# A graph network kernel: superblocks of destination nodes summed in pairs, and a fourteenth one by counted cells

## The reference, cut to what matters

```
msg = x[src] @ W_msg.T + b_msg + edge_embed[edge_type]
messages = segment_sum(msg, dst)             # (12500, 128)
x = layernorm(x + gru_cell(messages, x))     # W_ih, W_hh, b_ih, b_hh
h = x
for each of 3 layers:                        # with edge attributes, 16 wide
    agg = segment_sum(h[src] (+ or concat) (edge_attr @ enc_w + enc_b), dst)
    h = relu(bn(agg @ w1 + b1)) @ w2 + b2
out = layernorm(x + h)
```

## Time and profile before

| | |
|---|---|
| median of three runs | 7135.25 us |
| the profiled execution, and its span | 7139.24 us, 7137.2 us |
| share of the span busy | PE 82%, POOL 71%, DVE 46%, ACT 19% |
| busy tenths of PE in 40 slices | 2577777666677377767599999999999999999999 |
| busy tenths of the DMA engines in 40 slices | 6699999999999433333477778778878888778776 |

### The profile page before, as it was taken

The page is one execution under the profiler, slowest core; times in us unless marked ns, Lnnn a source line. Parts: engine busy times, 40 slices in busy tenths (PEclk is TensorE's granted clock), DMA queues, the critical chain, the costliest instruction groups (busy, mean ns, idle before and its releaser), DMA issues.

```text
span 7137.2 us, 82504 instructions
## 1 busy us (share of the span) xinstructions
PE 5870.9 (82%) x29016; PEld 2854.1 (40%) x29152; DVE 3267.2 (46%) x8030; ACT 1370.1 (19%) x2496; POOL 5097.1 (71%) x4958
## 2 busy tenths in 40 slices
PE   2577777666677377767599999999999999999999
PEld 1233333333333143333344444444455444445444
DVE  5666666655565486676544444432222222222222
ACT  1233333333334121121111111110000000000000
POOL 3766666666667477777577777777777777777775
PEclk9998898888989587777699999999999999999999
DMA  6699999999999433333477778778878888778776
GB/s 222 161 238 245 236 240 239 244 240 243 250 242 254 121 99 97 99 99 98 137 240 240 236 229 247 236 242 258 243 233 254 245 243 269 240 241 241 242 240 191
DMA packets 1463508, 1536.87 MB, mean 215 GB/s; under 512 B 820755, under 2 KB 1202772, under 8 KB 1463100
## 3 DMA queue, kind: packets, MB, share of 16 engines
q1 hardware_dynamic: 1250604, 1182.45, 58.4%
q0 software_dynamic: 212496, 349.08, 19.2%
HBM read 1082.27 MB, written 281.76 MB: 191 GB/s over the span
## 4 chain that ended last, share of the span: by engine, by line
PE 53%; POOL 5%; DVE 3%; DMA 2%; issue 2%; ACT 1%; SPq 0%; ACTq 0%; DVEq 0%
PE ps L2502 34%; PE ps L2473 6%; POOL BIG L2556 5%; PE ps L2447 2%; PE ps L2446 2%; PE ps L2359 1%; PE ps L2431 1%; PE ps L2360 1%; PE ps L2453 1%; DMA XT<-rec_q 1%; PE ps L2454 1%; PE ps L2398 1%; DVE BIG L1883 1%; PE ps L2361 1%; DMA RECL<-rec_q 1%
## 5 line engine op out<-in xcount | busy, mean ns | idle before, releaser
L2574 POOL DMA_INDIRECT GL<-h_gathered,IDXA x2646 | 2700.7, 1021 | 919.5 <-issue 770.4
L2502 PE MATMUL ps<-MS,HP 128*128 128x512 bf16 (+1 forms) x11700 | 2712.0, 376 | 27.8 <-DMA MS<-counts 16.1
L2541 POOL DMA_INDIRECT rec_q<-BIG x1563 | 1562.7, 1000 | 777.5 <-issue 470.2
L2502 PEld LDWEIGHTS ps<-MS,HP 128*128 128x128 bf16 x11700 | 1132.7, 98 | 1251.9 <-issue 117.1
L2300 PE MATMUL ps<-MT,XPS 128*128 128x512 bf16 x3763 | 1082.7, 397 | 490.8 <-ACT MT L2102 281.0
L2556 POOL DMA_INDIRECT BIG<-x_parts,SRCq x739 | 828.9, 1122 | 290.1 <-issue 222.8
L2102 ACT CAST MT<-ps 128x512 bf16<-128x512 f32 x1274 | 735.9, 586 | 971.3 <-PE ps L2286 823.9
L1960 DVE TENSOR_REDUCE ROW<-ps 128x128 f32<-128x384 f32 x294 | 163.0, 554 | 1517.6 <-PE ps L2473 1517.6
L2300 PEld LDWEIGHTS ps<-MT,XPS 128*128 128x128 bf16 x3822 | 373.7, 101 | 983.9 <-ACT MT L2102 433.5
L2473 PE MATMUL ps<-GL,SL 128*128 128x384 bf16 (+1 forms) x2646 | 593.9, 333 | 26.0 <-DVE SL L1926 26.0
L2286 PE MATMUL ps<-BIG 128*128 128x512 bf16 x1197 | 470.1, 393 | 44.6 <-DVE BIG L1748 30.1
(11 more groups left out here) (198 smaller groups left out, 4982.6 us busy)
## 6 DMA issues: line engine op xcount, KB each, us to landing
MS<-counts SPq DMA_DIRECT2D x936, 512.0 KB, 4.7
counts<-BIG SPq DMA_DIRECT2D x312, 512.0 KB
XPS<-x_parts SPq DMA_DIRECT2D x312, 384.0 KB, 5.0
GL<-h_gathered,IDXA POOLq DMA_INDIRECT x2646
rec_q<-BIG POOLq DMA_INDIRECT x1563
rec_q<-BIG SPq DMA_DIRECT2D x44, 490.0 KB, 15.2
HTI<-h_cols SPq DMA_DIRECT2D x72, 256.0 KB, 5.9
BIG<-rec_q SPq DMA_DIRECT2D x13, 980.0 KB, 6.5
```

Source lines behind the costliest of these rows:

```text
L2502: got = t.matmul(bank[:, 0:w].rearrange("p (b c) -> p b c", c=P), HP[:, d, part, :], MS[:, i % MR, 0:x.nb, d % MB, :], start=d + part == 0 ...
L2541: g.indirect_dma_start(out=RAd, out_offset=bass.IndirectOffsetOnAxis(ap=POSI[:, c:c + 1], axis=0), in_=RECA[q % 3][:, c - a, :], in_offset ...
L2574: g.indirect_dma_start(out=GL[:, r % LR, i, 0:3 * P], out_offset=None, in_=HGd[lay], in_offset=bass.IndirectOffsetOnAxis(ap=IDXA[:, a + i: ...
```

## The change

- The first layer's dense superblocks become 14 (JX = J + 1), while `counts` still has 13. Superblocks are taken in pairs: units alternate between the two superblocks of a pair with the same four source blocks, and one load of XPS serves both. There are 350 units and 175 XPS loads, against 325 and 325. The two superblocks of a pair are summed in PSUM banks 6 and 7.
- Superblock 13 has no cells of its own in `rec_q`. Its units take the first tile (k = 0 of K = 9) of each source block among the gathered edges, so each cell's piece of that load is one record of 80 bytes by itself. These 25 units are neither transposed nor stored.
- An edge of superblock 13 whose rank is over 128 is masked out in `window_places` (windows 13 and 14, three DVE instructions more in each).
- The records of cells come in halves of a pair: units 0 to 12 and 13 to 24 (HU = 13), two loads for each half.
- Units start one window later (after LAG), because a pair needs the windows of both superblocks; PACE is 50, so 16 or 17 units a window.
- In the first layer the gathered superblocks are 11: 675 gathers against 739, 226 dense and 169 gathered slots against 210 and 185. The order of groups ends with 24, 12, 13 (the last two dense), where it ended with 12, 24.

```diff
-JX = J
+JX = J + 1
-PACE = 44
+PACE = 50
+HU = 13
+class Unit:
+    def __init__(self, j, u, c0):
+        self.j, self.u, self.c0 = j, u, c0
+        self.n = min(4, NB - 4 * u)
+        self.pair = j // 2
+        self.load = SG * self.pair + u
+        self.half = 2 * self.pair + (u >= HU)
+        self.at = 4 * (u % HU)
+        self.first = j % 2 == 0
+        self.turn = None
+def units():
+    got, c = [], 0
+    for j in range(0, JX, 2):
+        for u in range(SG):
+            for k in range(j, min(j + 2, JX)):
+                got.append(Unit(k, u, c))
+                c += got[-1].n
+    for s, x in enumerate(x for x in got if x.j < J):
+        x.turn = s
+    return got
...
 def beside():
-            if w.q >= LAG:
+            if w.q > LAG:
                 work += PACE / w.groups
-            while m < SG * J and work >= (3 if m < SG * JX else 1) and m // SG <= w.q - LAG:
+            while m < len(UNITS) and work >= 3 and 2 * UNITS[m].pair + 1 <= w.q - LAG:
...
+            if w.q in (J, J + 1):
+                v.tensor_scalar(t1, DJ[:, sl], float(J), None, ALU.is_equal).then_inc(*dve.inc())
...
+                v.scalar_tensor_tensor(t1, r, 128.0, t1, ALU.is_gt, ALU.mult).then_inc(*dve.inc())
...
+                v.scalar_tensor_tensor(mk, t1, 0.5, mk, ALU.is_lt, ALU.mult).then_inc(*dve.inc())
...
         def cells_scalar(s, m):
             if m >= 3:
+                y = UNITS[m - 3]
+                if y.turn is not None:
+                    s.wait_ge(turn_out[y.turn % 2].sem, unit_turned(y.turn))
+                s.wait_ge(xd.sem, cells_to(m - 3))
...
         def sums_tensor(t, c):
+            m, i = CELLS[c]
+            x = UNITS[m]
+            if i == 0:
+                t.wait_ge(xps_in[x.load % 3].sem, 16 * (x.load // 3 + 1))
+            if 4 * x.u + i == 0 and x.j >= 2:
+                t.wait_ge(acc_out.sem, x.j - 1)
             for part in range(3):
+                got = t.matmul(PS[6 + x.j % 2][:, :], XPS[:, x.load % 3, i, part, :], MT[:, m % 3, 512 * i:512 * (i + 1)],
...
+        def cell_records_sync(y, k):
+            first = k // 2 * 2
+            if k % 2 == 0:
+                for q in range(max(0, first - 1), first + 3):
+                    y.wait_ge(scat[q % 3].sem, scattered(q))
+            if k >= 2:
+                y.wait_ge(ohs.sem, last_unit(lambda z: z.half == k - 2) + 1)
+            at, w = (0, 4 * HU) if k % 2 == 0 else (4 * HU, NB - 4 * HU)
+            for j in range(first, min(first + 2, JX)):
+                cells = RAv[:, NB * j:NB * (j + 1), :] if j < J else RAv[:, ND:ND + NS, :].rearrange("p (b k) w -> p b k w", k=K)[:, :, 0, :]
+                y.dma_start(RECS[k % 2][:, j % 2, 0:w, :], cells[:, at:at + w, :]).then_inc(*recs_in[k % 2].inc(16))
...
         def cells_sync(y, m):
+            x = UNITS[m]
+            if x.first:
+                if x.u == 4:
+                    cell_records_sync(y, 2 * x.pair + 1)
+                if x.u == 18 and 2 * x.pair + 2 < JX:
+                    cell_records_sync(y, 2 * x.pair + 2)
+                if x.load + 2 <= UNITS[-1].load:
+                    blocks_sync(y, x.load + 2)
...
+            if x.turn is None:
+                return
+            s = x.turn
+            y.wait_ge(mt_out.sem, cells_to(m))
+            y.dma_start(MST[s % 4][:, 0:4 * x.n, :], MT[:, m % 3, 0:512 * x.n], transpose=True).then_inc(*turn_out[s % 2].inc(16))
+            if s:
+                counts_out_sync(y, s - 1)
```

More of the change, by code:

```diff
@@ L133, with last_unit, cells_to @@
 CARRY = carries()
+class Unit:
[18 more added lines that the diff above has]
+    return got
+UNITS = units()
+TURNED = [x for x in UNITS if x.turn is not None]
+CELLS = [(m, i) for m, x in enumerate(UNITS) for i in range(x.n)]
+def last_unit(test):
+    return max(m for m, x in enumerate(UNITS) if test(x))
+def cells_to(m):
+    return UNITS[m].c0 + UNITS[m].n
 def beside():
@@ L148, in beside, with loaded, unit_turned @@
             at.append(here)
-    return at, list(range(m, SG * J))
+    return at, list(range(m, len(UNITS)))
 UNIT_AT, UNIT_REST = beside()
 XAT = {6 + 2 * i: i for i in range(SG)}
[L156 to L164, removed]
+def loaded(k):
+    return 16 * sum(min(2, JX - 2 * (e // 2)) for e in range(k % 2, k + 1, 2))
+def unit_turned(s):
+    return 16 * (s // 2 + 1)
 def scattered(q):
@@ L1471, in program @@
         RECA = [big(64 * RW).rearrange("p (c w) -> p c w", w=RW) for _ in range(3)]
[L1472 to L1474 removed]
+        recs0 = big(2 * 2 * 4 * HU * RW)
+        RECS = [recs0[:, 8 * HU * RW * i:8 * HU * RW * (i + 1)].rearrange("p (j c w) -> p j c w", j=2, w=RW) for i in range(2)]
+        DSF = [big(8 * HU).rearrange("p (j c) -> p j c", j=2) for _ in range(2)]
         OHS = [big(GT * 64).bitcast(BF16).rearrange("p (c b) -> p c b", b=P) for _ in range(3)]
@@ L2144, in sort_scalar @@
                 cells_scalar(s, m)
-            for j in range(J - 1, JX):
+            for j in range((JX - 1) // 2 * 2, JX):
                 sums_scalar(s, j)
@@ L2277, in cells_tensor @@
         def cells_tensor(t, m):
-            j, u, c0, n = unit(m)
+            x = UNITS[m]
             t.wait_ge(ohs.sem, m + 1)
-            for i in range(n):
-                c = c0 + i
+            for i in range(x.n):
+                c = x.c0 + i
                 t.wait_ge(ohd.sem, c + 1)
@@ L2317, in sort_tensor @@
                 cells_tensor(t, m)
-            for c in range(NB * J - 2, NB * JX):
+            for c in range(len(CELLS) - 2, len(CELLS)):
                 sums_tensor(t, c)
```

110 lines of the change are left out of this document (47 added, 63 removed).

## The result

The kernel after the change takes 7171.81 us, the median of four runs (7167.51 to 7173.46); the kernel before took 7136.97 beside it (four runs, 7131.29 to 7141.64). The ratio is 1.005, with a 95% interval of 1.0035 to 1.0065: slower by 0.5%, some 35 us, where 0.4% faster was forecast. The profiled execution took 7173.46 us, its span 7171.6, which is 34.4 us longer than that of before.

The account below looks back on a forecast made before the run. It took DMA transfers in SP's queue to bound the sort, POOL the first layer and PE the unchanged graph layers. Sort -9 and first layer -19 gave -28 us, 7111 in profile time, 7107 among the runs; range 7040 to 7165.

Parts of the forecast that it names:

- I take 1.3: Sort, SP's queue: each XPS load saved gives back 1.3 us, so a unit takes 4.97 us on average.
- a window takes 94.5 us, 0.4 more: Sort, windows 4 to 21: saved transfers are spent on two more units a window, +8 us over 18 windows.
- rival 3: Sort, SP's list: load worth 0.98 us, windows 97.2, 7155 (0.08); or transposes hold SP 4.4 us, windows 101.2, 7227 (0.07).
- Windows over 96 us: Sort, windows 4 to 21: sign that the forecast is wrong; SP's transposes with or without gaps tell the slower rivals apart.
- rival 2: Sort, windows 4 to 12: PE takes over, nine windows by +2.5 us, 7129, no measurable change; chance 0.16.
- The bounds of the load's price: Sort: an XPS load costs between its place on SP (0.43 us and 0.1) and 1.53 us by bytes; windows 92.6 and 101.2.
- the passage: Sort, between windows: 11.6 us a window beyond the units' pace, from a longer transpose interval and slow start; taken as unchanged.
- First transpose at 357: Sort's start: the first unit needs 64 more scatters, so its transpose comes at 357 us against 362.85, -6 us.
- Small pieces at 6 us: Sort, window 21: superblock 13's first 6656 pieces of 80 bytes cost +6 us, the second half nothing.
- Rival 4: Sort, queue before window 22: small pieces at a scatter's price, 110 us in place of 6, 7210; chance 0.03.
- The 5.6 and 4.3 us by turns: Sort, SP: sign that the forecast is right, transposes alternately 5.6 and 4.3 us apart.
- -19: Stage 2, first layer: 64 gathers less save POOL 91 us, of which 19 are gained; bounds 0 and -91.

Follow-up runs that it names:

- e2: Kernel after the change, with the 150 saved XPS loads put back into space nobody reads: 7306.90 us, ratio 1.0235 to the kernel before.
- e4b: Kernel after the change, with only the order of the first layer's groups changed (gathered spread among dense, 24 last): 7080.48 us, ratio 0.9906 to the kernel before.
- e4: Same group-order edit to the kernel after the change, on a chip slower as a whole: 9401.02 us, ratio 0.9987 to the kernel before.

## Why the prediction was wrong

**The step that failed: "I take 1.3" for an XPS load, and with it "a window takes 94.5 us, 0.4 more".** The load is worth 1.04 us by the intervals and 0.90 by e2. The windows take 97.0 us (97.3 by transposes), and the last place of window 21 came at 2083.25 and not at 2042. That is 41 of the 62 us between the forecast (-28) and the outcome (+34). Of the 2.5 us a window, 2.2 are the price (16.67 x 0.13) and 0.3 the error below. The mechanism was named right (SP's list, held by transfers in front, spends the saved load on more units), and rival 3's first case had both the price (0.98) and the window (97.2), with 0.08 of chance. Windows over 96 us were the forecast's own sign of being wrong, and its mark for rival 3 against rival 2 is there too: inside a window SP's list stands without a gap (1053.77 + 4.78 = 1058.55, the next entry is at 1058.59). The bounds of the load's price contained it; the upper of the two windows drawn from them, 101.2, comes to 100.9.

Why 1.3 was too much is known in part. The rate it was taken from isn't far off for the load itself: in the trace of before, between 450 and 2000 us, its 512 pieces of 768 B last 40.4 ns each, which is 1.29 us of the 16 engines. What failed is the step from there to the pace, that a transfer taken out of a full queue shortens it by its own time. Pieces overlap: without the passages the shares of the engines add up to 1.08, and 1.29/1.08 is 1.20. The rest of the way to 1.04 stays open. Nor does 0.98 come out for the reason that rival 3 gave: the 400 GB/s of the earlier trace rows are those of the stores of 490 KB, whose pieces are 3920 B.

**A second, smaller error in the same step.** I read 5.62 us a unit from four units in a good stretch. The mean over the stage is 5.78. The difference went into what I called the passage, as a fixed 11.6 us a window, but it grows with the units: 2 x 0.16 = 0.3 us of each window.

**The other steps of the sort held.** First transpose at 357 (356.87). Small pieces at 6 us: in the trace the 6656 pieces of 80 bytes run from 2025.3 to 2030.4, 5.1 us (that the 6 came so near is in part luck: 1.91 us was the issue of a transpose on an empty queue, and the 2048 pieces of that one ran 2.8 us), and SP's list waits behind them once, in the load that it issues next:

```profile
2016.38 3.76 SPq L2697 DMA_TRANSPOSE BIG<-MT  x1
2020.19 0.58 SPq L2704 DMA_DIRECT2D counts<-BIG  x1
2020.95 1.42 SPq L2656 DMA_DIRECT2D BIG<-rec_q  x2
2022.41 6.85 SPq L2667 DMA_DIRECT2D XPS<-x_parts  x1
2029.36 4.02 SPq L2697 DMA_TRANSPOSE BIG<-MT  x1
```

Rival 4's 110 us are out. A piece lasted 16.7 ns, the very price of the rival, but the 16 engines took them side by side. All that the engines moved in these 5.1 us comes to 134 GB/s, where it was 240 in the 5.3 us before. The Trainium skill, DMA: Bandwidth & Descriptors, Specifications, asks for pieces of 512 B and more for full rate. The trace agrees in the direction, and the price is small because the load is.

The last three windows are POOL's (297 us, 295 said). The 5.6 and 4.3 us by turns didn't come: in the rows above intervals are 5.50 (no load between) and 4.98 (with one), and between 450 and 2000 us they are 5.43 (128 of them) and 5.08 (123) in the mean. The queue averages over its entries, and only the sum of a pair, 10.5 us, can be read.

**Stage 2: "-19" was -2.6.** The part on POOL held to the microsecond: counted from the stage's start the last gather is at 1024.4 (1024 said). The tail was summed too short in two places. I let group 11 run beside the last gathers from 3334 on, but it had to wait for group 23, whose slots end at 3388.4 (3352 in the forecast's count), 18 us after 24's gathers begin: 24's slots end 15 us later than summed. And groups 12 and 13 take 86.5 us, not 82. Together 19 us, so the last slot stands where it stood before, less 3. My lower bound (0, if dense groups go at 45 us) was nearer than the value taken. The term that I put at nothing is the ring full for 66 us at the start, which the change left as it was: e4b gains 82 us of the stage by order alone, 24 in the gathers' span, where the ring was full, and 58 behind the last gather.

**The chances.** Faster had 0.61; the outcome lies 7 us above the range's upper end at 7165, in the 0.22 of slower. The price of a load had a measured row on either side, and the value taken was one that left a gain.

## What to carry to other kernels

Where a queue of transfers is the limit, price a transfer that goes by what the pace gives back when one is taken out or put in; here that was 0.90 to 1.04 us, less than the transfer's own time on the engines (1.3) and than its share by bytes (1.5). Take the bound that speaks against the change as a case of equal rank, and read a period as the mean over the whole stage. A change that frees one engine gains only what the last consumer can take: sum the tail after that engine's last instruction as carefully as the body. Before fitting more work into a full stage, look for a transfer whose place in an ordered list makes an engine wait (here 119 us for moving one load a window), and put added work where the full resource isn't full.

## What the runs showed of the hardware

- A DMA's issue time on SP was the pressure of the queue in front of it: the same transpose took 1.99 us at 356.87 and 4.78 at 1053.77, and an XPS load 0.44 us beside 6.85 behind the small pieces.
- A transfer taken from a full queue was worth 0.90 to 1.04 us, where by bytes it had 1.53 and its own pieces lasted 1.29 us of the 16 engines.
- The small pieces of the transposes took the largest part of the queue. Between 450 and 2000 us of the kernel before, a piece of 256 B (transposes) lasted 24.1 ns, one of 768 B (XPS loads) 40.4, one of 4096 B (stores of counts) 217. The transposes had 0.47 of the engines' time, the loads 0.20, the stores 0.28.
- Two chips were slower as a whole, by a third. In the waits of e4's kernel on one of them (450 to 2000 us) several engines stand for tens of us for what the profile calls remote (another core or a queue unknown to it), or for nothing that it shows; in the kernel after, on a usual chip, the only row of the first kind is ACT's, 88.3 us in 29 waits over the whole span, the longest 5.9. Single instructions take as long there as elsewhere (ACT's copy to MT 587 ns against 588 in e4b), and the DMA share from 600 to 1900 us is 0.59 against 1.01. What holds that chip back isn't known.

```profile
DVE CAR L1815 <- remote: 684.4, 21, 55.0
ACT MT L2153 <- remote: 663.8, 72, 36.6
PEld ps L2352 <- issue: 523.9, 203, 25.2
PE ps L2352 <- issue: 460.7, 67, 24.3
```

- One of four executions of e2's kernel took 23,595 us; it is in no comparison, and its cause is open.
